# A vision tower on one Trainium2 core: the last attention sorted by weight set, with gathered rows and weights taken by register

## The reference

```python
    routing_input = x.mean(axis=1)
    logits = jax.nn.relu(routing_input @ r_w1 + r_b1) @ r_w2 + r_b2
    sel = jnp.argmax(jax.nn.softmax(logits, axis=-1), axis=-1)
    params = [(wq0, wk0, wv0, wo0), (wq1, wk1, wv1, wo1), (wq2, wk2, wv2, wo2)]
    out = jnp.zeros_like(x)
    for i, nkv in enumerate(KV_OPTS):
        yi = gqa(x, *params[i], nkv)
        mask = (sel == i)[:, None, None]
        out = jnp.where(mask, yi, out)
    return out
...
h = h + _L3_ffn_ref(_layernorm(h, axis=-1), ...)
```

## Time and profile before

| | us |
|---|---|
| median of 3 runs (lowest, highest) | 1603.69 (1600.42, 1610.35) |
| the profiled execution, its time | 1606.4 |
| the profiled execution, its span in the trace | 1604.6 |

### The profile page before, as it was taken

One profiled execution on the slowest core, in us unless ns is written; L12 is line 12 of the kernel. 1 busy time (PEld: TensorE's weight loads), 2 busy tenths in 40 slices (PEclk: granted clock), 3 DMA queues, 4 the chain that ended last, 5 costly groups with the idle time before them and its releaser, 6 DMA issues. The chain is left out here.

```text
span 1604.6 us, 35141 instructions
## 1 busy us (share of the span) xinstructions
PE 1335.1 (83%) x11047; PEld 1161.7 (72%) x11047; DVE 807.8 (50%) x2632; ACT 737.7 (46%) x2600; POOL 352.2 (22%) x696
## 2 busy tenths in 40 slices
PE   6999579999964999462576999958997997589996
PEld 3777479999954999462575888848996886378884
DVE  0488531111144777437652555555332777557774
ACT  0588344444412555321242666624441786135553
POOL 0256411000010566413471000011000110110010
PEclk9999689999977999785697999979998899599998
DMA  6000010000001000002321000000000000100001
GB/s 225 13 1 0 1 34 27 13 26 13 0 1 40 2 0 0 14 1 64 116 48 51 1 0 0 1 9 25 20 7 32 2 0 1 38 1 1 0 0 31
DMA packets 27274, 34.49 MB, mean 21 GB/s; under 512 B 5673, under 2 KB 20212, under 8 KB 26932
## 3 DMA queue, kind: packets, MB, share of 16 engines
q1 hardware_dynamic: 22804, 26.13, 5.1%
q10 hardware_dynamic: 2784, 4.47, 0.8%
q0 software_dynamic: 1600, 2.82, 0.7%
HBM read 29.84 MB, written 4.03 MB: 21 GB/s over the span
## 5 line engine op out<-in xcount | busy, mean ns | idle before, releaser
L464 ACT ACTIVATE a_E<-quad_bank,a_shift 108x108 f32<-108x108 f32 x704 | 236.8, 356 | 3.9 <-DVE a_shift L528 3.4
L979 ACT ACTIVATE f_hid<-quad_bank,f_b1s 128x512 f32<-128x512 f32 (+1 forms) x240 | 148.0, 645 | 187.2 <-PE quad_bank L910 187.0
L1024 DVE SCALAR_TENSOR_TENSOR f_y<-bank,GATE,f_y 128x128 f32<-128x128 f32 x288 | 81.0, 344 | 253.0 <-PE bank L923 252.8
L923 PEld LDWEIGHTS bank<-f_w2s,f_hid 128*128 128x128 f32 x1728 | 201.7, 192 | 3.7
L923 PE MATMUL bank<-f_w2s,f_hid 128*128 128x128 f32 x1728 | 203.2, 275 | 0.0
L910 PE MATMUL quad_bank<-f_xp,f_w1p 128*128 128x512 f32 (+1 forms) x720 | 167.7, 382 | 16.6 <-DVE f_xp L1005 16.6
L910 PEld LDWEIGHTS quad_bank<-f_xp,f_w1p 128*128 128x128 f32 x720 | 125.1, 192 | 37.4 <-issue 8.5
L464 ACT ACTIVATION_READ_ACCUMULATOR a_E<-quad_bank,a_shift 108x1 f32 x704 | 150.3, 214 | 0.0
L358 PE MATMUL bank<-a_xT,a_wqk 128*128 128x108 f32 x1056 | 141.2, 286 | 1.4 <-ACT a_xT L482 1.4
L301 POOL TENSOR_TENSOR a_ve<-a_mv,const 108x1 f32<-108x1 f32 x88 | 16.7, 190 | 558.8 <-DVE a_mv L597 558.8
L358 PEld LDWEIGHTS bank<-a_xT,a_wqk 128*128 128x128 f32 x1056 | 131.9, 200 | 6.9 <-issue 4.3
(11 more groups left out here) (317 smaller groups left out, 2415.2 us busy)
## 6 DMA issues: line engine op xcount, KB each, us to landing
pats<-in_patches SPq DMA_DIRECT2D x3, 1296.0 KB, 18.5
pats<-in_patches ACTq DMA_DIRECT2D x2, 1296.0 KB, 15.0
f_w1s<-in_f_w SPq DMA_DIRECT2D x8, 256.0 KB, 2.7
f_w2s<-in_f_w SPq DMA_DIRECT2D x8, 256.0 KB, 3.2
f_w1a<-in_f_w SPq DMA_DIRECT2D x1, 2048.0 KB, 10.4
f_w2a<-in_f_w SPq DMA_DIRECT2D x1, 2048.0 KB, 14.8
out<-H SPq DMA_DIRECT2D x1, 1134.0 KB
a_f_in<-in_a_factors SPq DMA_DIRECT2D x1, 1088.0 KB, 5.6
```

The costliest lines, as they stand in the source:

```text
L464: e = act.activation(E[:, q, n, :], scores[:, n // tiles, n % tiles, :], ACT.Exp, scale=w.scale, bias=shift[:, q, n:n + 1], accum_out=tota ...
L923: mm = pe.matmul(m.bank[n % 2][0:W, g * D:(g + 1) * D], hid[:, n % 2, c, g * W:(g + 1) * W], w2s[:, u, c * 128:(c + 1) * 128], start=(c == ...
L979: act.activation(hid[:, n % 2, c, 0:k * W], m.quad_bank[:, (n * chunks + c) % 4, 0:k * W], func, bias=b1s[:, u, c:c + 1]).then_inc(hid_rea ...
L1024: ins = dve.scalar_tensor_tensor(out=h, in0=y[:, (g - c0) * D:(g - c0 + 1) * D], scalar=m.GATE[:, bass.ds(e + g * 8, 1)], in1=h, op0=ALU.m ...
```

## The change

- p4 also stores rows: SP writes all of `m.H` (6 DMAs) and, chunk by chunk, `m.XN` (6 DMAs) into a DRAM table of 2376 rows of 256 values: 128 normalised, 128 of the stream.
- `rt_w`, now larger, is loaded by SP behind a2's own weights (`early`), not in the router.
- `routes_phase` starts with 4 idle matmuls on PE. It no longer makes masks: it counts the images of each set, gives every image a slot such that each group of three slots holds one set only (NG = 23 groups, some slots empty), and writes the set of each group (`SET_OF`) and, for each group, the row numbers of its 108 tokens for reading and writing (`ROW_OF`; an empty slot is written nowhere).
- `routed_attention_phase` takes the place of a3 and of the storing block. Its pipeline has the same stages but for the norm (depth 4), over 23 groups. POOL gathers 108 rows of 1 KB per group, copies the stream's half into `a_h`, and scatters the result rows (512 B each) into `out`. SP reads the set of a group into a register and loads that set's weights from DRAM by three DMAs per group (256, 64 and 128 KB), in two buffers each. DVE adds the output into `a_h` once, and takes both halves of the maxima one behind the other.
- `attention_phase` loses `nx` and `masks`; for a0, a1 and a2 its instructions stay as they were.

```diff
-    first = (depth + 2) // 2 * 2
+def steps(eng, step, depth, count=G):
+    first = (depth + 2) // 2 * 2 + count % 2
...
-def attention_phase(nc, m, name, w, hd=HD, nx=1, ending="add", masks=False):
+def attention_phase(nc, m, name, w, hd=HD, ending="add", early=None):
...
-                    for x in range(nx):
-                        c = (4 * r + n) * 128
-                        mm = pe.matmul(qkbank[r][:, n * P:(n + 1) * P], wqk[:, x, c:c + 128], xT[:, par, x, :],
-                                       start=(x == 0 and (marked or not spare)), stop=(x == nx - 1), skip_group_check=True)
+                    c = (4 * r + n) * 128
+                    mm = pe.matmul(qkbank[r][:, n * P:(n + 1) * P], wqk[:, 0, c:c + 128], xT[:, par, :],
+                                   start=(marked or not spare), stop=True, skip_group_check=True)
...
+            if raw_rows is not None:
+                for c, k in CHUNKS:
+                    sp.dma_start(raw_rows[c * P:(c + k) * P, :].rearrange("(g p) d -> p g d", p=P),
+                                 m.H[:, c * D:(c + k) * D].rearrange("p (g d) -> p g d", d=D)).then_inc(rows_stored, 16)
...
+NG = (BATCH + SETS * (TB - 1)) // TB
...
-            sp.dma_start(rw[:, :], io["rt_w"]).then_inc(w_loaded, 16)
...
+            keep_busy(pe, m, m.bank[3], 4)
+            pe.wait_ge(m.rw_loaded, 16)
...
+            pe.wait_ge(chosen, 1)
+            flat = one[:, :, :].rearrange("p a x -> p (a x)")
+            pe.matmul(m.bank[2][0:B, 0:SETS], const("before"), flat, start=True, stop=True)
+            pe.matmul(m.bank[2][0:B, 8:8 + SETS], const("ones"), flat, start=True, stop=True).then_inc(psum, 1)
+            pe.wait_ge(placed, 1)
+            for i in range(TB):
+                mm = pe.matmul(m.bank[3][0:P, 0:NG], const("image")[:, i * P:(i + 1) * P], in_slot[:, i * NG:(i + 1) * NG],
+                               start=(i == 0), stop=(i == TB - 1))
+            mm.then_inc(psum, 1)
...
-            dve.tensor_tensor(spread[:, :, :], rw[0:B, 137 + P:137 + P + G].unsqueeze(2).broadcast_to([B, G, SETS]),
-                              one[:, :, :].broadcast_to([B, G, SETS]), ALU.mult).then_inc(spread_ready, 1)
+            dve.tensor_scalar(one[:, 0, :], one[:, 0, :], const("real"), None, ALU.mult).then_inc(chosen, 1)
             dve.wait_ge(psum, 3)
-            then(dve.tensor_copy(m.MSK[:, :], m.bank[2][0:P, 0:G * SETS]))
+            rank, totals = m.bank[2][0:B, 0:SETS], m.bank[2][0:B, 8:8 + SETS]
+            then(dve.tensor_tensor(over[:, :, :], totals.unsqueeze(2).broadcast_to([B, SETS, G]),
+                                   const("full").unsqueeze(1).broadcast_to([B, SETS, G]), ALU.is_gt))
+            then(dve.tensor_reduce(need[:, :], over[:, :, :], AX, ALU.add))
...
+            then(dve.tensor_reduce(at[:, :], spot[:, :], AX, ALU.add))
+            dve.tensor_scalar(in_slot[:, :], const("slot"), at[:, :], None, ALU.is_equal).then_inc(placed, 1)
+            then(dve.tensor_tensor(passed[:, :, :], const("group", 1).unsqueeze(2).broadcast_to([1, NG, SETS]),
+                                   until[0:1, :].unsqueeze(1).broadcast_to([1, NG, SETS]), ALU.is_ge))
+            then(dve.tensor_reduce(set_f[:, :], passed[:, :, :], AX, ALU.add))
+            then(dve.tensor_scalar(m.SET_OF[:, :], set_f[:, :], float(SETS - 1), None, ALU.min))
...
+            then(dve.tensor_scalar(m.ROW_OF[:, 0, :], image[:, :], float(S), const("token", P), ALU.mult, ALU.add))
...
+            then(dve.tensor_scalar(m.ROW_OF[:, 1, :], empty[:, :], const("token", P), None, ALU.add))
...
+def routed_attention_phase(nc, m, name, io, rows, stored, out):
...
+        wqk = sb("wqk", [128, 2, 4 * 128])
+        wv = sb("wv", [128, 2, NH * HD])
+        wo = sb("wo", [128, 2, tiles * D])
+        x = sb("x", [P, 2, 2, D])
+        h = sb("h", [P, NG, D])
...
+        def _(sp):
+            def load(j, dst, src, loaded, used_up, cols):
+                if 0 <= j < NG:
+                    e = sp.value_load(m.SET_OF[0:1, j:j + 1], min_val=0, max_val=SETS - 1)
+                    if j > 1:
+                        sp.wait_ge(used_up, j - 1)
+                    sp.dma_start(dst[:, j % 2, :], src[bass.ds(e, 1)].rearrange("e p n -> p (e n)")).then_inc(loaded[j % 2], 16)
+            for j in range(NG + 3):
+                load(j, wqk, io[name + "_wqk"], wqk_loaded, qk_psum, 512)
+                load(j - 1, wv, io[name + "_wv"], wv_loaded, v_psum, 128)
+                load(j - 3, wo, io[name + "_wo"], wo_loaded, y_psum, 256)
+        @block.gpsimd
+        def _(pool):
+            def gather(j):
+                pool.indirect_dma_start(out=x[:, j % 2, :, :].rearrange("p a d -> p (a d)"), out_offset=None, in_=rows[:, :],
+                                        in_offset=bass.IndirectOffsetOnAxis(ap=m.ROW_OF[:, 0, j:j + 1], axis=0)).then_inc(gathered[j % 2], 16)
+            def scatter(j):
+                pool.wait_ge(y_done, j + 1)
+                if j > 1:
+                    pool.wait_ge(scattered[j % 2], 16 * (j // 2))
+                pool.indirect_dma_start(out=out[:, :], out_offset=bass.IndirectOffsetOnAxis(ap=m.ROW_OF[:, 1, j:j + 1], axis=0),
+                                        in_=h[:, j, :], in_offset=None, bounds_check=BATCH * S - 1,
+                                        oob_is_err=False).then_inc(scattered[j % 2], 16)
+            pool.wait_ge(stored, 2 * 16 * len(CHUNKS))
+            gather(0)
+            gather(1)
+            for j in range(NG):
+                pool.wait_ge(gathered[j % 2], 16 * (j // 2 + 1))
+                pool.tensor_copy(h[:, j, :], x[:, j % 2, 1, :]).then_inc(h_here, 1)
+                if j + 2 < NG:
+                    pool.wait_ge(h_here, j + 1)
+                    pool.wait_ge(xt_psum, j + 1)
+                    gather(j + 2)
+                if j > 2:
+                    scatter(j - 3)
+            for j in range(NG - 3, NG):
+                scatter(j)
+            for u in range(2):
+                pool.wait_ge(scattered[u], 16 * len(range(u, NG, 2)))
...
+                if on(t, 0):
+                    pe.wait_ge(gathered[par], landed(t, par))
+                    at_least(pe, v_ready, t - 1)
+                    pe.transpose(xbank[:, 0:P], x[:, par, 0, :], m.ident[0:P, 0:P]).then_inc(xt_psum, 1)
...
+                    pe.wait_ge(wo_loaded[q], landed(g, q))
+                    for tile in range(tiles):
+                        mm = pe.matmul(xbank[0:P, 0:D], oT[:, tile * P:(tile + 1) * P], wo[:, q, tile * D:(tile + 1) * D],
+                                       start=(tile == 0), stop=(tile == tiles - 1))
+                    mm.then_inc(y_psum, 1)
...
+                    pe.wait_ge(wqk_loaded[par], landed(t, par))
+                    for n in range(4):
+                        mm = pe.matmul(qkbank[:, n * P:(n + 1) * P], wqk[:, par, n * 128:(n + 1) * 128], xT[:, par, :], start=True, stop=True)
+                    mm.then_inc(qk_psum, 1)
...
+                    pe.wait_ge(wv_loaded[q], landed(g, q))
+                    pe.matmul(xbank[0:P, 0:NH * HD], xT[:, q, :], wv[:, q, :], start=True, stop=True).then_inc(v_psum, 1)
...
-        prepare_phase(nc, m, "p4", means=True)
-        routes_phase(nc, m, io)
-        w = Weights(io["a3_wv"], HD ** -0.5, io["a3_wqk"], io["a3_wo"])
-        attention_phase(nc, m, "a3", w, nx=SETS, masks=True)
...
-                sp.dma_start(dst, h[:, 0:full, :]).then_inc(stored, 16)
-                sp.dma_start(out[full * TB:BATCH].rearrange("b s d -> (b s) d"),
-                             h[0:(BATCH - full * TB) * S, full, :]).then_inc(stored, 16)
-                sp.wait_ge(stored, 32)
+        rows = nc.dram_tensor("a3_rows", (G * P, 2 * D), F32).ap()
+        stored = prepare_phase(nc, m, "p4", means=True, rows=rows[:, 0:D], raw_rows=rows[:, D:2 * D])
+        routes_phase(nc, m)
+        routed_attention_phase(nc, m, "a3", io, rows, stored, out.rearrange("b s d -> (b s) d"))
```

357 lines of the change are left out of this document (278 added, 79 removed).

## The result

The changed kernel takes 1535.9 us, the median of 4 runs (1532.4 to 1539.4), against 1604.2 for the kernel before (4 runs, 1600.4 to 1610.4): a ratio of 0.9553, with a 95% interval from 0.9519 to 0.9588. The forecast was 1536. The profiled execution took 1539.4 us, 1.8 more than its span.

A forecast was written before the change was run, and what follows sets the result against it. PE alone was taken to bound the last attention's steady part; terms +5.3 - 2.3 - 8.1 - 56.4 - 6.5 = -68.0 us, from the median 1603.7 gave 1535.7, forecast 1536 us, with an 8-in-10 range of 1520 to 1556.

The forecast's parts named there:

- p4 and the table's load: p4's row stores and the table's load moved into a2: 0 us, or 3 or so if the stores' cover were gone.
- Routes: Router ahead of a3: idle matmuls start it 1.5 us later, a longer chain adds 3.8; together +5.3, bounds +2 and +8.
- Start of a3: From a3's idle matmuls to its first transpose: 10.2 us instead of 12.5, the norm being gone; -2.3, bounds -4 and 0.
- Fill: From a3's first transpose to first `a_oT`: 15.0 us instead of 23.1, -8.1; 13 at full clock; other end 22.4, -0.7.
- Steady part: a3's repeated group steps: 22 intervals of 4.7 us, 103.4 against 159.8, so -56.4; bounds 93 and 117.
- the model from a2: a2, the same pipeline with one weight set, taken as model of the new step: 4.73 us per group.
- rival 3: a3's steady part reaches its lower bound, PE alone setting a 4.3 us step: -9 us, so 1527; chance 0.24.
- Tail: From the last `a_oT` to the end: 7.1 us instead of 13.6, so -6.5, bounds -8 and -4.
- block end and clearing, about 2.5: Within the tail: the block's end and semaphore clearing after the last scatter lands, about 2.5 us, taken from the kernel before.
- Rival 1: a3's steady part: new transfers on SP or POOL bound the step at 5.4 us, +15, so 1551; chance 0.13.
- Rival 2: The new attention's clock falls to 1.2 GHz and stays: step 8.2 us, +77 and fill +7, so 1620; chance 0.03.
- The issue on POOL beside VectorE's copies: a3's steps: each POOL DMA issue could lose up to a VectorE copy's length; small loss expected, nothing changed in the sum.

The follow-up runs named there:

- experiment 1: The kernel before with one weight set instead of three in the last attention, no sorting or gather: 1543.6 us, ratio 0.9607.
- experiment 4: The changed kernel with a norm's work put back on VectorE in each step, ahead of `a_recs`: 1554.6 us, ratio 0.9682.
- experiment 7: The changed kernel without the clearing of semaphores after the last attention: 1554.9 us, ratio 0.9633 (condition B).
- experiments 2 and 3: The changed kernel with SP's register loads replaced by a fixed set: 1538.9 us, ratio 0.9572; with each register load done twice: 1539.0 us, ratio 0.9586.
- experiment 6: The changed kernel with 9 idle matmuls instead of 14 at a3's start: 1554.3 us, ratio 0.9613; with none: 1557.4, ratio 0.9651 (condition B).
- condition A: Runs in which the kernel before took 1604 and 1606 us; the changed kernel took 1535.9 us, ratio 0.9553.
- condition B: Two later series in which the kernel before took 1616 and 1619 us; the unaltered changed kernel took 1557.0 us, ratio 0.9608.

## Why the prediction was right, point by point

- **Median.** 1536 predicted, 1535.9 measured. The sum of the terms for the profiled execution was 1538.4, against 1539.4, and this rests on errors that cancel: +2.2 ahead of p4 (not from the change), steady -3.9, fill -1.3, tail +3.7.
- **p4 and the table's load.** Costed at 0; POOL issued its first gather 0.8 us after a3's start and waited for no stored row. Right.
- **Routes.** +5.3 predicted (idle matmuls +1.5, chain +3.8), +5.4 measured (+1.4 and +4.0). Right.
- **Start of a3.** 10.2 us predicted, 10.3 measured. Right.
- **Fill.** 15.0 predicted, 13.7 measured: it ran at full clock from its first transpose, near the 13 that I had named for that case. The 7.0 us that I had put down to fewer matmuls need the clock: with one set and the old norm ahead of the first transpose it was at half, and the fill took 22.4 (experiment 1). So the choice between my two ends, 15.0 and 22.4, made for the shorter pause, carried the term.
- **Steady part.** 4.7 us a step predicted, 4.52 measured. The mis-sized term is the model from a2: "4.73, with two falls of the clock in it". In the trace of after, a2 itself took 4.59 without such falls, so 0.14 of the 0.18 us is the clock. Against that a2 the first steps are 0.1 longer (4.53 against 4.43), which is what I had put for the real matmul of the values, and the loop's shorter (4.53 and 4.70 against 4.59 and 4.96). The latter fits rival 3, in which VectorE is relieved, but no run took the norm alone away. "PE alone bounds it" was too short for the new step: TensorE is busy 98% of it, and still 0.8 us more of VectorE between `a_h` and `a_recs` made it 5.1 (experiment 4).
- **What the gain is made of.** I had put the steady part down to matmuls alone. One set without sorting has a step of 5.0 us (experiment 1), so 2.6 of the 3.1 us per group came without the sorting, by the matmul work and the two of three mask operations that went with it. The other 0.5 are, by difference, what the change takes off VectorE (norm, mask) and the new order of its list, which no run told apart; nearly all of it stands in the loop's steps, 0.1 in the written-out ones.
- **Tail.** 7.1 predicted, 10.8 measured. "After the last sum on `a_h` the span ends within 6 us" is wrong: 9.4. The step that failed is "block end and clearing, about 2.5", taken from a stretch of before with a block's end and its clearing. Product and sum took 1.5 as costed (2.0). POOL began the scatter 0.85 us after the sum, which I had not counted, and needed 0.99 for it; the last packets moved by 1530.9, and 6.7 us followed, of which the clearing is 2.4 and POOL's drain at the block's end 3.8 (experiment 7). Before, a3's block had no such drain; that of f1, which ends behind POOL's indirect DMAs, had one of 5.6, and it was the row to cost this block's end by. Why the drain takes so long behind them is not shown.
- **Rival 1** fell: 3.3 us of SP in 4.5, and 1.7 us more make it true (experiments 2 and 3). **Rival 2** fell: full clock throughout the steady part, and even without idle matmuls (experiment 6). **Rival 3**, a step of 4.3, was not reached.
- **The issue on POOL beside VectorE's copies.** I had said that f1's mean of 1.0 us speaks for a small loss. In condition A there was none. In condition B the time is lost on VectorE, not on POOL: 0.5 us a step, 110.3 us for the 22 intervals against 99.5. My term, 103.4, would have been 7 us short there.

## What to carry to other kernels

Take the pace of a new stage from an existing one of the same form, as was done here, but take out the falls of the clock first, and look for engines whose list is full at one place though they are busy three quarters of the time: 0.8 us of VectorE ahead of `a_recs` cost 0.6 and more in a 4.5-us step, while a2 has its norm elsewhere in the list and steps of 4.4 to 5.0. Read the written-out steps and those of a loop apart. Idle matmuls put in to raise the clock are worth a run without them: in condition B both sets cost more than they gave. Cost the end of a block in which POOL issued indirect DMAs by another such block of the same trace. And a kernel that issues DMAs from POOL in its inner loop should be timed more than once, some time apart and on more than one chip: here the same code had two steps.
